# Gated attention on one core: queries and keys projected transposed, values packed 17 columns a head, zeros written during attention, group 0 loaded during the projections

## What is computed

```python
xn = _layernorm(x)                                   # per position, over 256 features
q, k, v = split_heads(xn @ W_q), split_heads(xn @ W_k), split_heads(xn @ W_v)   # 16 heads of 16
q, k = _apply_rope(q, cos, sin), _apply_rope(k, cos, sin)
    # x * cos + concat([-x2, x1]) * sin, x1 and x2 the two halves of a head's 16 features
scores = jnp.where(causal, -jnp.inf, q @ k^T)
s = (softmax(scores / sqrt(16)) @ v).reshape(b, s, 256) @ W_o
expert = argmax(softmax(xn @ w_router.T))            # one of 8 experts per position
h = xn @ w_fc[expert].T                              # 128 hidden
h = where(h >= 0, h, 0.5 * h) ** 2
g = silu(h @ w_proj[expert].T)
out = x + s * g
```

## Time and profile before

| | |
|---|---|
| median of 3 runs | 2648.99 us (2640.83 to 2650.19) |
| the profiled execution | 2668.93 us, its span 2667.2 us |
| PE, DVE, ACT, POOL busy | 95%, 80%, 67%, 37% of the span |
| granted TensorE clock, mean | 0.975 |
| moved by DMA | 435.04 MB |
| projections, first to last rope product | 19.5 to 404.4 us |
| first row matmul of attention | 445.5 us |
| last mask of attention | 2291.3 us |

### The profile page before, as it was taken

The page is one execution under the profiler, slowest core; times in us unless marked ns, Lnnn a source line. Parts: engine busy times, 40 slices in busy tenths (PEclk is TensorE's granted clock), DMA queues, the critical chain, the costliest instruction groups (busy, mean ns, idle before and its releaser), DMA issues. The chain is left out here.

```text
span 2667.2 us, 53565 instructions
## 1 busy us (share of the span) xinstructions
PE 2530.6 (95%) x16876; PEld 1274.2 (48%) x16877; DVE 2136.1 (80%) x6183; ACT 1782.9 (67%) x4187; POOL 988.9 (37%) x1187
## 2 busy tenths in 40 slices
PE   7999993999999999999999999999999999899777
PEld 6878781333333333333333333333333333588666
DVE  7888886888888888888888888888888888354344
ACT  5777770677777777777777777777777777655111
POOL 6888884222222222222222222222222222222665
PEclk9999995999999999999999999999999999999888
DMA  7999998446556456455457465455464561597997
GB/s 240 351 347 354 353 328 194 103 96 112 106 99 113 94 100 116 97 103 115 89 106 151 88 108 110 89 111 114 90 116 100 93 111 38 170 310 274 299 320 218
DMA packets 305865, 435.04 MB, mean 163 GB/s; under 512 B 101808, under 2 KB 204464, under 8 KB 305584
## 3 DMA queue, kind: packets, MB, share of 16 engines
q1 hardware_dynamic: 293296, 398.05, 58.1%
q0 software_dynamic: 12288, 33.57, 5.6%
HBM read 241.18 MB, written 188.74 MB: 161 GB/s over the span
## 5 line engine op out<-in xcount | busy, mean ns | idle before, releaser
L884 DVE CUSTOM_DVE_ANT_0 dump<-ps_rows,mask 128x512 bf16<-128x512 f32 (+7 forms) x2048 | 1481.2, 754 | 224.4 <-issue 185.4
L863 ACT ACTIVATE probs<-ps_cols 128x512 f32<-128x512 f32 (+3 forms) x3072 | 1315.8, 495 | 514.5 <-PE ps_cols L1032 503.9
L1032 PE MATMUL ps_cols<-q_st,k_st 99*128 99x512 bf16 (+3 forms) x3072 | 863.3, 329 | 5.5 <-DMA q_st<-max_T 3.3
L842 POOL TENSOR_SCALAR_AFFINE_SELECT probs<-probs 128x512 f32<-128x512 f32 x512 | 325.9, 636 | 1363.8 <-ACT probs L863 1363.8
L976 PE MATMUL ps_rows<-k_st,q_st 96*128 96x512 bf16 (+3 forms) x3072 | 781.7, 331 | 29.5 <-DMA v_st<-v_dram 21.9
L1008 PE MATMUL ps_ctx<-probs,v_st 128*32 128x512 f32 (+3 forms) x6144 | 655.2, 498 | 1.5 <-POOL probs L842 1.3
L1032 PEld LDWEIGHTS ps_cols<-q_st,k_st 99*128 99x128 bf16 x3072 | 279.8, 97 | 591.0 <-ACT probs L863 380.8
L976 PEld LDWEIGHTS ps_rows<-k_st,q_st 96*128 96x128 bf16 x3072 | 265.3, 98 | 326.5 <-DVE row_max L884 127.8
L1008 PEld LDWEIGHTS ps_ctx<-probs,v_st 128*32 128x32 f32 x6144 | 120.9, 108 | 206.5 <-issue 103.3
L280 POOL TENSOR_TENSOR roped<-rope_c,rope_s 128x512 f32<-128x512 f32 x128 | 165.0, 1289 | 41.0 <-DVE rope_s L404 40.8
L884 DVE DVE_READ_ACCUMULATOR2_ANT row_max<- 128x1 f32 x2048 | 168.7, 82 | 0.2
(11 more groups left out here) (113 smaller groups left out, 2669.6 us busy)
## 6 DMA issues: line engine op xcount, KB each, us to landing
parts_dram<-parts SPq DMA_DIRECT2D x128, 384.0 KB, 3.8
q_st<-parts_dram SPq DMA_DIRECT2D x384, 128.0 KB
k_st<-parts_dram SPq DMA_DIRECT2D x384, 128.0 KB
v_dram<-v_sb SPq DMA_DIRECT2D x128, 256.0 KB, 5.2
v_st<-v_dram SPq DMA_DIRECT2D x64, 512.0 KB
xs_dram<-zeros SPq DMA_DIRECT2D x36, 512.0 KB, 6.9
xs_sb<-xs_dram SPq DMA_DIRECT2D x72, 256.0 KB, 4.9
g_dram<-g_sb SPq DMA_DIRECT2D x72, 256.0 KB, 3.5
```

What stands on the lines that cost most here:

```text
L842: nc.gpsimd.affine_select(out=tri, in_=tri, compare_op=ALU.is_ge, fill=0.0, base=0, pattern=[[0, GH], [1, P]], channel_multiplier=-1).then ...
L863: nc.scalar.activation(probs[:, k % PB, h, 0:w], ps_cols[(GH * k + h) % CB][:, 0:w], ACT.Exp).then_inc(exp_done, 1)
L884: nc.vector.tensor_tensor_reduce(out=dump[:, even, 0:n], in0=ps_rows[:, 512 * bank:512 * bank + n], in1=mask[:, S - n:S], scale=1.0, scala ...
L1032: nc.tensor.matmul(ps_cols[(GH * k + h) % CB][:, 0:w], k_st[r][:, j // IB, h * 512 + (j % IB) * P:h * 512 + (j % IB + 1) * P], q_st[r][:, ...
```

## The change

- **Queries and keys transposed.** The weights are now the stationary operand and the transposed xn of a whole tile the moving one, so a matmul gives 128 features x 512 positions. Loops run over m = 2t + a, with a = 0 for queries and 1 for keys; each has two banks, one for the first and one for the second halves of all 16 heads (four banks, two m). The rotation multiplies whole banks; POOL subtracts and adds. `transpose_qk` is gone. The three parts are cut 1024 elements at a time. ACT and DVE now read the rotated values from SBUF.
- **Order.** PE: values of the first sub of m, for keys the transposes of xn subs 2 and 3 of the next tile, the first bank, values of the second sub, for queries the transposes of xn subs 0 and 1, the second bank. POOL: both adds of m, part3 of m - 2, and for keys `scale(t + 2)` (the former `rstd_of`).
- **Weights** are cut into high and low in five pieces, in a new column order; the scale of the queries moves from the table into the DVE instruction; the table is smaller.
- **Values** take 17 columns a head (16 and a one); a matmul still reads 32, which reach into the next head. The tile's values are stored by one DMA, the parts by two.
- **Zeros** for xs_dram are written in attention, four DMAs in each of the first nine groups; the scatters follow in the other 55 groups.
- **Group 0** has its operands outside of both phases; its 13 loads are issued by SP at tile 8. The causal mask and both identities are made in the projections.
- **onehot** is written in its own order, no longer through a transposed view.

```diff
+def load_operands(sp, parts_dram, v_dram, b, r, q, k, v, loaded):
+    for a, (dst, slots) in enumerate(((q, SLOT_Q), (k, SLOT_K))):
+        for slot, part in enumerate(slots):
+            src = parts_dram[:, a, part].rearrange("(b c) (d g h) t -> b g d c (h t)", c=TPB, g=NG, h=GH)[b, r]
+            sp.dma_start(dst[slot * HD:(slot + 1) * HD], src).then_inc(loaded, 16)
+    src = v_dram[:, r].rearrange("(b c) p n -> b p c n", c=TPB)[b]
+    sp.dma_start(v[:, 0:NB * V_ROW].rearrange("p (c n) -> p c n", c=TPB), src).then_inc(loaded, 16)
...
     @block.sync
...
-            for i in range(CLEARS * t // NT, CLEARS * (t + 1) // NT):
-                clear_xs(i)
+            if t > 0:
+                store_parts(t - 1)
+            if t == FIRST_GROUP_AT:
+                for j in range(TPB):
+                    sp.wait_ge(v_stored[j % 2], 16 * (j // 2 + 1))
+                    sp.wait_ge(parts_stored[j % 2], 32 * (j // 2 + 1))
+                load_operands(sp, parts_dram, v_dram, 0, 0, *first_in)
...
     @block.gpsimd
...
+        def turn(m):
+            u = m % 2
+            pool.wait_ge(half_turned, m + 1)
+            if m >= 2:
+                pool.wait_ge(rest_ready, m - 1)
+            nc.gpsimd.tensor_tensor(roped[:, u, 0], rope_c[:, u, 0], rope_s[:, u, 0],
+                                    ALU.subtract).then_inc(roped_ready, 1)
+            pool.wait_ge(qk_used, 2 * m + 2)
+            nc.gpsimd.tensor_tensor(roped[:, u, 1], rope_c[:, u, 1], rope_s[:, u, 1],
+                                    ALU.add).then_inc(roped_ready, 1)
+        def part3(m):
+            t, a = divmod(m, 2)
+            pool.wait_ge(part2_done, m + 1)
+            nc.gpsimd.tensor_tensor(parts[:, t % 2, a, 2], rest[:, m % 2], parts[:, t % 2, a, 1],
+                                    ALU.subtract).then_inc(part3_done, 1)
+        for m in range(NM + 2):
+            if m < NM:
+                turn(m)
+            if m >= 2:
+                part3(m - 2)
+            if m % 2 == 1 and m // 2 + 2 < NT:
+                scale(m // 2 + 2)
...
     @block.scalar
...
+        for m in range(NM + 2):
+            t, a = divmod(m, 2)
+            if m < NM:
+                values(2 * m)
+                if t + 1 < NT:
+                    if a == 0:
+                        apply(t + 1, 0)
+                        apply(t + 1, 1)
+                    else:
+                        xT_hi(t + 1)
+            if m >= 2:
+                part2(m - 2)
+            if m < NM:
+                values(2 * m + 1)
+                if a == 0 and t + 1 < NT:
+                    apply(t + 1, 2)
+                    apply(t + 1, 3)
+            if 1 <= m <= NM:
+                part1(m - 1)
...
     @block.vector
...
+        def rotate(m):
+            t, a = divmod(m, 2)
+            u, at = m % 2, (t % TPB) * TOK
+            cos, sin = (rope_sb[:, i, at:at + TOK] for i in range(2))
+            first, second = ps_qk[2 * u], ps_qk[2 * u + 1]
+            def times(out, ps, table):
+                if a == 0:
+                    return nc.vector.scalar_tensor_tensor(out, ps[:], SCALE, table, ALU.mult, ALU.mult)
+                return nc.vector.tensor_tensor(out, ps[:], table, ALU.mult)
+            if m >= 2:
+                dve.wait_ge(roped_ready, 2 * (m - 1))
+            dve.wait_ge(qk_ready, 2 * m + 1)
+            times(rope_c[:, u, 0], first, cos)
+            times(rope_s[:, u, 1], first, sin).then_inc(qk_used, 1)
+            dve.wait_ge(qk_ready, 2 * m + 2)
+            times(rope_s[:, u, 0], second, sin).then_inc(half_turned, 1)
+            times(rope_c[:, u, 1], second, cos).then_inc(qk_used, 1)
+        def take_rest(m):
+            t, a = divmod(m, 2)
+            dve.wait_ge(part1_done, m + 1)
+            if m >= 2:
+                dve.wait_ge(part3_done, m - 1)
+            nc.vector.tensor_tensor(rest[:, m % 2], roped[:, m % 2].rearrange("p k t -> p (k t)"),
+                                    parts[:, t % 2, a, 0], ALU.subtract).then_inc(rest_ready, 1)
+        for m in range(NM + 1):
+            t, a = divmod(m, 2)
+            if m < NM:
+                if a == 1 and t + 1 < NT:
                     xT_lo(t + 1)
+                rotate(m)
                 if t + 2 < NT:
+                    if a == 0:
+                        ln_stats(t + 2)
+                    else:
+                        ln_scale(t + 2)
+            if m >= 1:
+                take_rest(m - 1)
...
-        nc.vector.tensor_tensor(onehot[:].rearrange("p e s -> p s e"),
-                                first_best[:].unsqueeze(2).broadcast_to((P, NS, E)),
-                                ids_low[:].unsqueeze(1).broadcast_to((P, NS, E)), ALU.is_equal).then_inc(route, 1)
+        nc.vector.tensor_tensor(onehot[:], first_best[:].unsqueeze(1).broadcast_to((P, E, NS)),
+                                ids_low[:].unsqueeze(2).broadcast_to((P, E, NS)), ALU.is_equal).then_inc(route, 1)
...
     @block.tensor
...
+        def heads(m, k):
+            t, a = divmod(m, 2)
+            cols = slice((2 * a + k) * P, (2 * a + k + 1) * P)
+            if m >= 2:
+                pe.wait_ge(qk_used, 2 * (m - 2) + k + 1)
+            three_passes(ps_qk[2 * (m % 2) + k][:], lambda i, c: w_all_hl[i][:, c, cols],
+                         lambda j, c: xT_hl[j][:, t % 2, c, :]).then_inc(qk_ready, 1)
...
+        for m in range(NM):
+            t, a = divmod(m, 2)
+            pe.wait_ge(xT_lo_ready, DC * (t + 1))
+            values(2 * m)
+            if a == 1 and t + 1 < NT:
+                transpose_xn(t + 1, (2, 3))
+            heads(m, 0)
+            values(2 * m + 1)
+            if a == 0 and t + 1 < NT:
+                transpose_xn(t + 1, (0, 1))
+            heads(m, 1)
...
 def attention_phase
...
     @block.sync
...
+            if n < CLEAR_GROUPS:
+                for i in range(CLEARED // 2):
+                    clear_xs(CLEARED * n + i)
             store_ctx(n, b, r, 0)
             if not last:
                 load_max(n + 1, (r + 1) % RING, 0)
...
+            if n < CLEAR_GROUPS:
+                for i in range(CLEARED // 2, CLEARED):
+                    clear_xs(CLEARED * n + i)
...
     @block.gpsimd
...
         for r in range(RING):
             nc.gpsimd.memset(k_st[r][KS:KM], 1.0).then_inc(ones_set, 1)
+        pool.wait_ge(ones_set, RING)
+        for r in range(1, RING):
+            nc.gpsimd.memset(v_st[r][:, NB * V_ROW:], 0.0).then_inc(ones_set, 1)
+        pool.wait_ge(ones_set, 2 * RING - 1)
+        nc.gpsimd.memset(zeros[:], 0.0).then_inc(zeros_set, 1)
```

More of the change, by code:

```diff
@@ L105, in project_phase @@
     xT_hl = [sb(f"xT_{n}", [P, 2, DC, TOK], F32R) for n in ("hi", "lo")]
[L106 to L113, removed]
+    rope_c = sb("rope_c", [P, 2, 2, TOK])
+    rope_s = sb("rope_s", [P, 2, 2, TOK])
+    roped = sb("roped", [P, 2, 2, TOK])
+    rest = sb("rest", [P, 2, 2 * TOK])
+    v_sb = sb("v_sb", [P, 2, NG, SUB, V_ROW])
+    parts = sb("parts", [P, 2, 2, PARTS, 2 * TOK], BF16)
     logits = sb("logits", [P, NS, E])
@@ L139, in project_phase @@
     ps_f = [bank(f"ps_f{i}") for i in range(2)]
-    ps_qk = [bank(f"ps_qk{i}") for i in range(2)]
+    ps_qk = [bank(f"ps_qk{i}") for i in range(4)]
     ps_vr = [bank(f"ps_vr{i}") for i in range(2)]
-    ps_m = [bank(f"ps_m{i}") for i in range(2)]
     x_loaded = [sem(f"x_loaded{u}") for u in range(XR)]
@@ L407, in take_rest @@
-        def take_rest(n):
-            t, s = divmod(n, SUB)
-            dve.wait_ge(part1_done, n + 1)
-            if n >= RR:
-                dve.wait_ge(part3_done, n - RR + 1)
-            nc.vector.tensor_tensor(rest[:, n % RR].rearrange("p (b t) -> p b t", b=4),
-                                    ps_m[n % 2][:].rearrange("p (b t) -> p b t", b=4),
-                                    parts[:, t % 2, :, 0, s * P:(s + 1) * P], ALU.subtract).then_inc(rest_ready, 1)
-        for n in range(NS + LAG):
-            t, s = divmod(n, SUB)
-            if n < NS:
-                if s == SUB - 1 and t + 1 < NT:
+        def rotate(m):
[15 more added lines that the diff above has]
+            times(rope_c[:, u, 1], second, cos).then_inc(qk_used, 1)
@@ L593, in attention_phase @@
     xn_sb = sb("xn_sb", [P, 2, SUB, D])
+    zeros = sb("zeros", [P, 4 * D])
     RB = 4
@@ L730, in attention_phase, with subs_scattered @@
     block = ctx.enter_context(nc.Block())
-    LOAD = 16 * (2 * len(SLOT_Q) + 1)
-    SUBS_SCATTERED = NT * SUB // N
+    CLEARS = NBLK * BLK // (4 * P)
+    CLEAR_GROUPS = 9
+    CLEARED = CLEARS // CLEAR_GROUPS
+    def subs_scattered(n):
+        at = [NT * SUB * max(m - CLEAR_GROUPS, 0) // (N - CLEAR_GROUPS) for m in (n, n + 1)]
+        return range(*at)
     SCATTER_STEP = IB
@@ L738, in load @@
         def load(b, r):
[L740 to L747 removed]
+            load_operands(sp, parts_dram, v_dram, b, r, q_st[r], k_st[r], v_st[r], operands_loaded[r])
         def load_max(n, r, c):
```

365 lines of the change are left out of this document (153 added, 212 removed).

## The result

The changed kernel took 2828.1 us (median of 4 runs, 2826.3 to 2833.4), the kernel before beside it 2645.9 (2640.8 to 2650.2): ratio 1.0693, 95% interval 1.0665 to 1.0720. It is slower by 182 us; predicted were 2826 us and +177.

What follows compares the result with a forecast made beforehand. POOL's program order and the DVE products feeding it were taken to set 12.12 us a projection tile. Loop +194, start +0.5, routing -3.5 and +0.8, handoff -15.1 gave +177 on 2649: 2826 us, range 2720 to 2868.

Steps and rivals of the forecast that it cites:

- The chain: Projections loop: scale, shift, xn, transposes, query matmuls and DVE and POOL work follow one another, 15.5 us a tile.
- The port: Projections loop: take_rest's two SBUF inputs and POOL exclude each other, +0.6 and +1.1 us a tile, making 17.2.
- rivals without exclusion: Projections loop: no exclusion at the port while the clock falls, 1.7 us a tile less, 2774 us; chance 0.10.
- POOL always first: Projections loop: POOL is always served first at the port, 0.8 us a tile more, 2850 us; chance 0.07.
- The clock: Projections loop: TensorE falls to 1.2 GHz in its pause, slowing matmuls and transposes, 17.2 to 18.7 us a tile.
- Loop sum: Projections loop: 29 periods of 18.7 us plus lighter ends, 584 us against 389.6 before, +194 us.
- rival with neither port nor clock: Projections loop: neither exclusion at the port nor a falling clock, 2725 us; chance 0.08.
- Start: Before the loop: weights cut in five pieces, some +1, with a shorter ScalarE wait for constants; +0.5 us.
- Routing: Routing after the loop: contiguous onehot saves 3.5 us; POOL's last 1024-wide part3 holds L435 0.8 us longer.
- Handoff: Projections to attention: group 0 and constants already in SBUF, so rows start at 430.4; -15.1 us.
- Attention: Attention: moved zeros, later scatters and 17-column values cost 0 us, at most 18 for zeros if cover is gone.
- rival of the hidden chain: Projections loop: chain hidden but port not, 12.7 us a tile, +19, with the handoff 2651 us; chance 0.05.

Runs made afterwards that it cites:

- exchanged work: Changed kernel with VectorE doing the rotation's adds and GpSimd take_rest: 2728.7 us; with GpSimd's scale also half a tile earlier: 2634.4 us.
- PE kept busy: Changed kernel with GpSimd's scale half a tile earlier, plus ten unused matmuls a tile where TensorE waited for xT_lo: 2681.2 us.
- scale early: Changed kernel with GpSimd's scale(t+2) and VectorE's ln_scale half a tile earlier: 2719.8 us.
- early, one input: Changed kernel with GpSimd's scale half a tile earlier and take_rest given one SBUF input, its subtraction left out: 2681.5 us.

## Why the prediction held, step by step

**The chain** (15.5 us a tile, predicted). The measured tile of 18.75 less the port (1.63) and the clock (1.34), each taken away alone, leaves 15.8, if the two add up. The late scale as its cause is shown from two sides: earlier scale 3.65 us less in the profiled execution (in the faster one, by the 48.5 us above, an estimated 5.4), later transposes 2.7 less; and with the exchanged work, 15.3 against 11.94.

**The port** (1.7). 1.63 when the second SBUF input is gone. The size held, the second place did not: I had the second take_rest come during POOL's first add and go ahead of the second; it came with the second add (308.04, 307.99), ended 1.1 us behind it and went ahead of part3, which took 1.0 us longer for it. The rivals without exclusion (2774) and with POOL always first (2850) fall: at 301.80 and 308.04 VectorE was served between two instructions of POOL. The Trainium skill (SBUF — State Buffer, "Who interferes with whom") says it is an exclusive lock for VectorE's two-input instructions against GpSimd's reads; the trace agrees, each stands still until the other's instruction has ended (part3 3029 against 2143 ns).

**The clock** (1.5). 1.34. PE went to the half level in the pause before the transposes, and the stretch shows 0.83, as a third of the time at half.

**Loop sum** +194: +197.3. (The terms as given, 542 + 3 + 13 + 10 + 17, make 585 and not 584; and by the 29 periods the rival with neither port nor clock comes to 2733, not 2725. Neither changes the reading.) **Start** +0.5: +0.4. **Routing** -3.5 and +0.8:
```profile
608.02 2.12 POOL L323 TENSOR_TENSOR parts<-rest,parts 128x1024 bf16<-128x1024 f32 x1 [2.25 <-ACT parts L374]
608.09 3.13 DVE L496 TENSOR_TENSOR is_best<-logits,best 128x1024 f32<-128x1024 f32 x1
...
613.77 1.22 DVE L504 TENSOR_TENSOR onehot<-first_best,ids_low 128x1024 bf16<-128x1024 f32 x1
```
onehot 1.22 for 4.70, is_best 3.13 for 2.13: -3.5 and +1.0; here too VectorE ends one full duration after POOL. **Handoff** -15.1: -15.2 from the sum, 15.7 from the run without it. **Attention** 0: 0. The move of the zeros and the narrower values were not run by themselves; the unchanged 1845.8 us is what stands for them.

**Where I erred.** I announced POOL idle for 3.5 to 5 us a tile ahead of its first add; it is 99.5/19 = 5.2, and 20.2/19 = 1.1 ahead of the other half's first. That figure did not follow from my own sum, 18.7 less 10.4 of work and some 2 of stops. And I had POOL wait at its second add; in fact its adds kept their 1.26 to 1.29 us, and it waits at part3, which takes 3.1 us for 2.1, in both halves. "At most 10, once" for group 0's loads was 0 here and 10.8 as soon as a tile took 11.3: the rival of the hidden chain would have paid it. That rival itself (12.7 a tile) came close to what the early scale gives with PE kept busy, 12.45; with the early order alone I had expected it and got 15.1, because I had not seen that a stop ahead of xT_lo makes a new pause of PE.

## What to carry to other kernels

Follow one item around its cycle through all engines and write down each queue it stands in, before comparing work per engine: PE lost 16 transposes a tile and the kernel lost 7%, more than half of it because LayerNorm's small pair stood last in GpSimd's program (3.65 or more of the 6.6 us a tile). Where VectorE and GpSimd both run in a loop, give VectorE the work that has an input in PSUM and GpSimd the SBUF-to-SBUF work; here that, with the early scale, made 15.1 us a tile into 11.9. Loads moved into a stage were free here only while that stage was slow; spread one a tile they cost less.

## What the hardware showed unexpectedly

- A VectorE instruction on 4 elements (L426, tensor_scalar, one SBUF input) took 2.18 us behind GpSimd's part3, mean 1.5 us over 18 tiles of the run scale early, 0.16 undisturbed. In the run early, one input the tile's time went with it: 11.4 to 11.6 us without that stop, 14.1 to 15.6 with it. So one SBUF input does not always free it, while tensor_reduce with one input of 1024 elements never took over 1.22 us. The Trainium skill (SBUF — State Buffer, "Who interferes with whom") names tensor_scalar among the operations that can take both ports, and tensor_reduce as one that does not on trn2; the rows agree.
- More work on TensorE made the kernel faster: 24 useless matmuls a tile, -34 us.
- One kernel ran at 2720 us three times and 2672 once on the same chip, at a mean granted clock of 0.957 and 0.975.
